# Taps loaded from ScalarE's DMA queue instead of SyncE's, in a depthwise convolution over normalized groups

## What is computed

```python
# x: (32, 384, 56, 56) float32, weight: (384, 1, 56, 1), bias: (384,)
def _L0_conv_ref(x, weight, bias):
    x_cat = jnp.concatenate([x, x[:, :, :-1, :]], axis=2)
    out = jax.lax.conv_general_dilated(x_cat, weight, (1, 1), 'VALID',
              dimension_numbers=('NCHW', 'OIHW', 'NCHW'), feature_group_count=384)
    return out + bias[None, :, None, None]

def _gn(v, G=32, eps=1e-5):          # 32 groups of 12 channels, mean and variance per image and group
    ...
    return ((g - m) / jnp.sqrt(s + eps)).reshape(v.shape)

x = x + _L0_conv_ref(_gn(x), weight, bias)
```

## Time and profile before

| what | value |
|---|---|
| median of three runs | 801.14 us (800.21 to 803.91) |
| the profiled execution's own time | 799.6 us |
| its span, first to last instruction | 797.8 us |
| TensorE busy | 690.0 us, 86% of the span |
| VectorE (DVE) busy | 713.8 us, 89% |
| ScalarE (ACT) busy | 673.1 us, 84% |
| GpSimd (POOL) busy | 583.9 us, 73% |
| DMA: moved, mean rate | 316.09 MB, 396 GB/s |

### The profile page before, as it was taken

One profiled execution on the slowest core, in us unless ns is written; L12 is line 12 of the kernel. 1 busy time (PEld: TensorE's weight loads), 2 busy tenths in 40 slices (PEclk: granted clock), 3 DMA queues, 4 the chain that ended last, 5 costly groups with the idle time before them and its releaser, 6 DMA issues.

```text
span 797.8 us, 9115 instructions
## 1 busy us (share of the span) xinstructions
PE 690.0 (86%) x1920; PEld 557.9 (70%) x1920; DVE 713.8 (89%) x1602; ACT 673.1 (84%) x1029; POOL 583.9 (73%) x1110
## 2 busy tenths in 40 slices
PE   0599999898899888998988998888898989988895
PEld 0477877776677667776776777777776767776784
DVE  7899999998998899999989999999888999989962
ACT  6799998888889888898888898888887888897893
POOL 4688787777677667687777677677786777776775
PEclk9999999999999999999999999999999999999999
DMA  9979999999999999999999999999999999999956
GB/s 343 409 301 375 410 410 418 424 418 417 416 416 414 414 426 412 413 404 402 405 417 418 412 402 400 411 412 410 402 409 406 409 407 399 410 406 403 375 239 251
DMA packets 43784, 316.09 MB, mean 396 GB/s; under 512 B 12816, under 2 KB 12944, under 8 KB 14992
## 3 DMA queue, kind: packets, MB, share of 16 engines
q1 hardware_dynamic: 43728, 315.51, 97.4%
HBM read 161.32 MB, written 154.14 MB: 395 GB/s over the span
## 4 chain that ended last, share of the span: by engine, by line
DMA 41%; SPq 16%; DVE 16%; POOL 10%; ACT 8%; issue 6%; PE 2%; POOLq 0%
DMA xt<-x 29%; DVE st L311 9%; DMA out<-xt 8%; SPq L190 7%; SPq L172 7%; POOL xt L278 6%; ACT xn L387 6%; DVE xt L336 4%; DMA runs<-taps 3%; ACT kept L396 2%; PE conv L462 2%; DVE runs L320 1%; DMA xt<-wide 1%; SPq L179 1%; SPq L183 1%
## 5 line engine op out<-in xcount | busy, mean ns | idle before, releaser
L462 PE MATMUL conv<-xn,runs 128*128 128x448 f32 x1536 | 645.3, 567 | 38.4 <-ACT xn L387 36.7
L462 PEld LDWEIGHTS conv<-xn,runs 128*128 128x128 f32 x1536 | 514.1, 346 | 101.9 <-ACT xn L387 58.5
L278 POOL TENSOR_TENSOR xt<-xt,kept 128x448 f32<-128x448 f32 x384 | 436.7, 1144 | 97.8 <-ACT kept L396 97.4
L387 ACT ACTIVATE xn<-xt,shift,rstd 128x672 f32<-128x672 f32 x512 | 462.8, 942 | 44.6 <-POOL shift L272 44.6
L311 DVE BATCH_NORM_STATS2 st<-xt 128x6 f32<-128x336 f32 x1024 | 451.9, 494 | 54.1 <-DMA xt<-x 49.4
L336 DVE SCALAR_TENSOR_TENSOR xt<-conv,bias_all,xt 128x448 f32<-128x448 f32 x384 | 256.8, 669 | 18.0 <-PE conv L462 18.0
L396 ACT ACTIVATE kept<-conv,bias_all 128x448 f32<-128x448 f32 x384 | 234.2, 620 | 10.7 <-PE conv L462 9.8
L438 PEld LDWEIGHTS p_mean<-msum,neg_mean 128*128 128x128 f32 x128 | 19.5, 192 | 94.3 <-POOL msum L247 79.5
L438 PE MATMUL p_mean<-msum,neg_mean 128*128 128x8 f32 x128 | 25.2, 269 | 59.2 <-POOL msum L247 59.2
L377 ACT ACTIVATE std<-var,eps 128x8 f32<-128x8 f32 x64 | 19.3, 301 | 54.5 <-DVE var L326 54.0
L268 POOL TENSOR_TENSOR newt<-r 128x8 f32<-128x8 f32 x64 | 12.7, 198 | 49.9 <-DVE r L331 48.2
(11 more groups left out here) (29 smaller groups left out, 111.6 us busy)
## 6 DMA issues: line engine op xcount, KB each, us to landing
xt<-x SPq DMA_DIRECT2D x128, 672.0 KB, 7.5
out<-xt SPq DMA_DIRECT2D x128, 672.0 KB, 6.8
xt<-x SPq DMA_DIRECT2D x128, 336.0 KB, 7.6
out<-xt SPq DMA_DIRECT2D x128, 336.0 KB, 6.9
out<-xt SPq DMA_DIRECT2D x128, 168.0 KB, 12.0
xt<-x SPq DMA_DIRECT2D x124, 168.0 KB, 12.4
runs<-taps SPq DMA_DIRECT2D x32, 192.0 KB, 10.9
xt<-wide SPq DMA_DIRECT2D x4, 336.0 KB, 7.2
```

The costliest lines, as they stand in the source:

```text
L278: nc.gpsimd.tensor_tensor(cell, cell, kept_of(u, c), ALU.add).then_inc(pool_added, 1)
L387: ins = nc.scalar.activation(xn[:, n % NS, :, part], xt[0:P, n % XS, :, part], ACT.Identity, scale=rstd[:, n % RS, b:b + 1], bias=shift[:, ...
L462: nc.tensor.matmul(bank(c), lay[:, :, c], channel_of(xn, u % NS, c), start=True, stop=True).then_inc(conv_ready, 1)
```

## The change

The transfers of taps are issued by ScalarE, on its own DMA queue. Those of groups 0 and 1 come at the start, behind its zeroing of two slots and a wait for the zeroed `runs`. Those of group g + 2 come behind the last eviction of the second unit of group g. SyncE keeps x, the bias and the result, and no longer waits for `runs_zeroed`. Buffers, sizes and semaphores of the transfers stay as they were.

```diff
@@ block.sync
-            def load_taps(g):
-
-                sp.dma_start(runs[0:SIDE, g % 2, 0:BLOCK], taps[g]).then_inc(taps_loaded[g % 2], 16)
-
...
-            sp.wait_ge(runs_zeroed, 1)
-            load_taps(0)
             sp.dma_start(bias_all[:], bias).then_inc(bias_loaded, 16)
             for n in range(2, XS):
                 sp.wait_ge(slot_zeroed[n], 1)
                 for h in range(HALVES):
                     load(n, h)
-                if n == 3:
-                    load_taps(1)
 
             for u in range(UNITS):
                 for h in range(HALVES):
                     store(u, h)
-                    g = u // PER_GROUP + 2
-                    if h == 1 and u % PER_GROUP == PER_GROUP - 1 and g < GROUPS:
-                        load_taps(g)
-
                     if u >= 1:
                         load(u - 1 + XS, h)
@@ block.scalar
+            def load_taps(g):
+                nc.scalar.dma_start(runs[0:SIDE, g % 2, 0:BLOCK], taps[g]).then_inc(taps_loaded[g % 2], 16)
+
...
             for n in (2, 3):
                 nc.scalar.memzero(xt[:, n, :, :]).then_inc(slot_zeroed[n], 1)
+            act.wait_ge(runs_zeroed, 1)
+            for g in range(2):
+                load_taps(g)
             act.wait_ge(consts_set, 2)
...
                 for c in ACT_CH[4:]:
                     evict(u, c)
+                g = u // PER_GROUP + 2
+                if u % PER_GROUP == PER_GROUP - 1 and g < GROUPS:
+                    load_taps(g)
```

## The result

The changed kernel takes 795.06 us (median of four runs, 793.64 to 795.61) against 801.95 for the kernel before (four runs): a ratio of 0.9928, with a 95% interval of 0.990 to 0.9955. That is 0.7% faster. The time lies in the stated range, but it is not the forecast of 800.5: rival (b), 795.5, came closest.

What follows compares the result with a forecast made beforehand. The full DMA queue was taken to bound the kernel from 110 to 750 us; +1.0 + 0.3 − 2 = −0.7 on 799.6 gave 798.9, stated as 800.5 us on the median's scale, range 791 to 811.

Steps and rivals of the forecast that it cites:

- (b): Long stretch: the disturbance by passing taps goes away, −6.9 + 1.3 = −5.6 us, giving 795.5 us; chance 0.16.
- What bounds the kernel: Transfers set the pace from 110 to 750 us, DMA share 1.01 at 411 GB/s; compute before, then a 48 us drain.
- SyncE loses 32 issues: 0: SyncE, whole kernel: dropping issues of 0.59 to 1.3 us lets loads be issued sooner, but is worth nothing.
- ScalarE's issues: 0 and +0.3: 30 issues behind a group's last eviction: 0 in the long stretch, +0.3 us for three issues before 110 us.
- Two transfers at the start: between 0 and +1.4, taken as +1.0: Start: taps of groups 0 and 1 slip ahead of unit 1's last piece of x, delaying the end by +1.0 us.
- Thirty transfers beside SyncE's queue: −2 of at most −6.9: Loop's taps on their own queue: disturbance of 0.23 us each shrinks; −2 us taken, between −6.9 and +8.1.
- By it the −2 would be 0: Loop's 30 transfers: by the skill, issuing from several engines saves only sequencer time, so the −2 us would be 0.
- (c): Long stretch: the late rate recovers as well, to some 425 GB/s, −21 us, about 780 us; chance 0.08.
- (d): Long stretch: the disturbance grows, every passing as bad as the worst window, +8.1 + 1.4 + 0.3, 811 us; chance 0.14.
- (e): ScalarE's issues are held by SyncE's full queue; an issue of 4 us would give 844 us; chance 0.05.
- (f): Transfers are served in order of issue, taps find the same place, only the start is spared: 801 us; chance 0.08.
- The signs: Expected in the profile: ScalarE's own queue, taps landing in 3 to 5 us, first convolution up to 1.4 us later.

Runs made afterwards that it cites:

- experiment 2: Against the kernel before: the loop's taps on ScalarE, the start's on SyncE, SyncE issuing small transfers where it issued taps; 792.61 us, ratio 0.9877.
- experiment 3: The kernel before without the loop's 30 transfers of taps, all groups using the matrices of groups 0 and 1; 773.84 us, ratio 0.9667.
- late kernel of experiment 5: Against the kernel before: ScalarE issues the loop's taps behind its second eviction of the next unit, start on SyncE; 789.98 us, ratio 0.9843.
- early kernel: The kernel before with SyncE issuing the loop's taps ahead of the second half's store, after a wait for the last product; 807.4 to 831.9 us, ratio 1.0133.

## Why the prediction was right or wrong

- *What bounds the kernel*: right. The share of 1.01 in the long stretch stayed, and the profile gave no new kind of wait for ScalarE or SyncE (SyncE's wait for GpSimd before a store went from 148.5 to 168.9 us).
- *SyncE loses 32 issues: 0*. Right, shown by putting them back (experiment 2).
- *ScalarE's issues: 0 and +0.3*. The 0 was right. An issue takes 0.473 us, less than the row of SyncE it was taken from, and the 0.81 us of idle time stayed. The issue starts ahead of the evictions that it stands behind, so it does not even need that idle time. The +0.3 before 110 us is not shown by itself: in the changed kernel unit 8 is as late as the first convolution, 2.2 us, and with the loop's transfers alone its square root comes at 107.73 us, 0.7 late.
- *Two transfers at the start: between 0 and +1.4, taken as +1.0*. The mechanism was right, the size wrong: +2.2 us in the profile, +2.0 in the experiment. The step that failed is "behind its two zeroings, which end at 11.28 us". ScalarE issued at 4.13 us, when its first zeroing still ran and the second had not begun, so the transfers met x of unit 0 too: the later first statistics and the waits of 1.60 and 0.42 us cost 2.55 us, of which 2.19 are left at the statistics that had started at 17.61. The rule of turns between queues in the Trainium skill, "DMA: Bandwidth & Descriptors", section "Queues, rings and completion order", by which the term was +1.4, had the direction, and the trace agrees that taps of the new queue passed x of the old one.
- *Thirty transfers beside SyncE's queue: −2 of at most −6.9*. This term decided the case, and both its size and its bound were too small: −9.5 us measured for the loop alone, and −12.6 to −14 were to be had. My windows began 5 us after each issue, while the mean dip lies 2 to 8 us after it, so half of it was counted into the pieces "between"; the 0.23 us a transfer are really 0.42 (experiment 3). That made the bound too small. And the choice of −2 rested on "its partitions and sizes are the same", when it was the partitions that made the cost, and a second queue makes the dip short even so.
- *"By it the −2 would be 0"* (the Trainium skill, "DMA: Bandwidth & Descriptors", section "Issuing engines are not separate DMA queues", by which issuing from several engines only saves sequencer time). Here it does not hold: the sequencer's time was worth nothing, and the second queue was worth 1.2 to 1.6%. With the rows spread, where 0.9825 on SyncE's queue and 0.9809 on ScalarE's agree, it does.
- *Rivals.* (b) had the mechanism and nearly the number, if by two errors that offset: −6.9 for the loop and +1.3 for the start, against −9.5 and +2.0. (c), a full recovery of the late rate to some 425, is seen in a small part: from 600 to 740 us the rate is 411 GB/s after the change and 414 with the late issue, against 406 before. (d) and (e) did not come. (f) is excluded by the start, where taps passed x issued before them, and by the late kernel of experiment 5.
- *The signs.* The second queue, the full long stretch and the late first convolution came. Taps landed after 7.3 us, not 3 to 5; the first convolution was 2.2 us late, not up to 1.4; the wait for shift did not get shorter.
- *The chances.* The case within 0.5% had 0.57; the result lies beyond it by two tenths of a per cent. The range held because (b) was in it, not because the sum was right.

## What to carry to other kernels

When the transfers are the bound, look at the rate in the stretch where a small transfer passes, not only at its bytes and its landing time; find the dip by averaging over all passes before choosing windows. A load to 64 neighbouring partitions amid a full queue can cost about as much again as its bytes (here 0.42 us beside 0.47). Putting its rows on every second partition took that away here, and a queue of its own, with the layout as it was, took most of it (9.5 to 12.6 us of 14). Do not let such transfers loose on a free queue at the very start, though: here they overtook the data that the first unit waits for, and cost 2.2 us.

## What the hardware showed that I had not expected

- ScalarE issues a transfer while earlier work of its own is still running, and even before it has begun: at 4.13 us under a zeroing that lasts to 6.71, and at 168.51 us ahead of the evictions that start at 169.02.
- Where the 192 KB transfers of taps go was worth from −1.7% (every second partition, the old place in SyncE's queue) to +1.3% (neighbouring partitions, the early place), though they are 2% of the bytes.
- In the profiled execution of the early kernel, the longest, the loss builds up over hundreds of us, from 422 to 378 GB/s. What accumulates was not settled.
